# The output bias of three attentions as one more product in the projection's accumulation

## The reference, cut to what matters

```python
def _L2_xattn_ref(query, key, value, Wq, bq, Wk, bk, Wv, bv, Wo, bo):
    q, k, v = query @ Wq + bq, key @ Wk + bk, value @ Wv + bv     # split into 16 heads
    scores = jnp.einsum('bhqd,bhkd->bhqk', q, k) / jnp.sqrt(HEAD_DIM)
    attn = jax.nn.softmax(scores, axis=-1)
    out = jnp.einsum('bhqk,bhkd->bhqd', attn, v)                  # heads joined again
    return out @ Wo + bo

x = x + jnp.tanh(g_xattn[2]) * _L2_xattn_ref(_layernorm(x), ctx_1024, ctx_1024, ...)
```

## Time and profile before

| | us |
|---|---|
| three runs | 1636.18, 1635.72, 1634.01 |
| median | 1635.72 |
| profiled execution: time | 1638.06 |
| profiled execution: span of the trace | 1636.3 |
| PE busy in the span | 1386.8 (85%) |
| DVE busy | 1240.5 (76%) |
| ACT busy | 772.5 (47%) |
| POOL busy | 337.0 (21%) |

### The profile page before, as it was taken

How to read it: one execution, slowest core, us unless ns; L and a number is a source line. 1 busy time by engine, 2 the same in 40 slices (tenths; PEclk the granted TensorE clock), 3 DMA queues, 4 the chain that set the end, 5 groups by cost and what they waited for, 6 DMA issues and landing times.

```text
span 1636.3 us, 25886 instructions
## 1 busy us (share of the span) xinstructions
PE 1386.8 (85%) x9890; PEld 1266.5 (77%) x9890; DVE 1240.5 (76%) x2386; ACT 772.5 (47%) x1318; POOL 337.0 (21%) x278
## 2 busy tenths in 40 slices
PE   4897997798995599999399459968998999999995
PEld 4786895586883599999379358966886888999995
DVE  5696778777896589997379779976886857888773
ACT  4445442113455266666355442325445225676673
POOL 2241001000000157764100000000000013454342
PEclk9898998799998599998699879988998999999997
DMA  4232100000002478886300000000002016777784
GB/s 139 91 104 89 45 1 1 1 0 10 1 1 110 150 211 233 244 224 174 124 1 1 7 0 1 1 10 1 1 1 104 1 65 233 233 214 220 219 241 116
DMA packets 44926, 148.23 MB, mean 91 GB/s; under 512 B 11651, under 2 KB 22582, under 8 KB 35062
## 3 DMA queue, kind: packets, MB, share of 16 engines
q1 hardware_dynamic: 28886, 122.04, 21.9%
q0 software_dynamic: 15936, 24.78, 7.8%
HBM read 126.03 MB, written 22.87 MB: 91 GB/s over the span
## 4 chain that ended last, share of the span: by engine, by line
PE 56%; DVE 26%; ACT 8%; issue 5%; DMA 2%; POOLq 1%; SPq 1%; POOL 0%; ACTq 0%; DVEq 0%
PE PS L307 37%; PE PS L1005 6%; PE PS L966 3%; PE PS L989 3%; DVE RA L1624 2%; PE PS L1240 1%; DVE RA L1693 1%; ACT Y L225 1%; ACT RA L1617 1%; DVE FA L1661 1%; PE PS L998 1%; DVE RA L297 1%; PE PS L982 1%; DVE RA L1673 1%; POOLq L2764 1%
## 5 line engine op out<-in xcount | busy, mean ns | idle before, releaser
L307 PE MATMUL PS<-RA 128*128 128x256 f32 (+3 forms) x6204 | 942.7, 311 | 74.9 <-DVE RA L397 16.2
L307 PEld LDWEIGHTS PS<-RA 128*128 128x128 f32 x6204 | 859.5, 197 | 130.3 <-issue 34.5
L1551 POOL DMA_INDIRECT sum_rows<-Y,KT x78 | 158.6, 2033 | 193.1 <-ACT Y L1592 162.2
L271 POOL TENSOR_TENSOR rstd<-vareps,neghalf 128x4 f32<-128x4 f32 x36 | 36.8, 1023 | 707.2 <-DVE vareps L208 330.0
L1005 PE MATMUL PS<-VBF,FA 128*128 128x136 f32 x1024 | 136.1, 287 | 4.4 <-ACT FA L771 4.2
L1540 POOL DMA_INDIRECT Y<-normed_rows,KT x78 | 89.8, 1151 | 219.7 <-DVE KT L1333 158.5
L1005 PEld LDWEIGHTS PS<-VBF,FA 128*128 128x128 f32 x1024 | 124.8, 192 | 10.3 <-ACT FA L771 6.8
L771 ACT ACTIVATE FA<-PS 128x1024 f32<-128x1024 f32 x64 | 65.7, 1027 | 103.9 <-PE PS L966 103.9
L1570 ACT ACTIVATE FA<-PS,unit_bias 128x256 f32<-128x256 f32 (+1 forms) x184 | 71.7, 445 | 78.2 <-PE PS L307 65.4
L1624 DVE TENSOR_TENSOR RA<-FA,RA 128x2048 fp32r<-128x2048 f32 x46 | 105.2, 2288 | 4.4 <-ACT RA L1584 3.7
L1693 DVE TENSOR_TENSOR RA<-FA,RA 128x1024 fp32r<-128x1024 f32 (+1 forms) x46 | 80.9, 1759 | 24.8 <-ACT RA L1617 24.8
(11 more groups left out here) (295 smaller groups left out, 1874.9 us busy)
## 6 DMA issues: line engine op xcount, KB each, us to landing
FA<-in_eup SPq DMA_DIRECT2D x46, 1024.0 KB, 7.0
FA<-in_edown SPq DMA_DIRECT2D x23, 1024.0 KB, 6.3
FA<-in_edown SPq DMA_DIRECT2D x23, 512.0 KB, 4.1
FA<-in_fside SPq DMA_DIRECT2D x16, 512.0 KB, 3.6
sum_rows<-X SPq DMA_DIRECT2D x2, 2048.0 KB, 7.4
normed_rows<-Y SPq DMA_DIRECT2D x2, 2048.0 KB, 10.2
fp_rows<-FA POOLq DMA_DIRECT2D x6, 352.0 KB, 6.8
FA<-fp_rows SPq DMA_DIRECT2D x1, 2112.0 KB, 11.9
```

The lines of the kernel that those rows point to most:

```text
L307: ins = pe.matmul(dst, stat(a, k), mov(b, k), start=(first and n == 0), stop=(last and n == len(todo) - 1))
L1551: pool.indirect_dma_start(out=sum_rows, in_=rows_out[p][:, t, :], in_offset=None, compute_op=ALU.add, out_offset=bass.IndirectOffsetOnAxis ...
```

## The change

In layers 1 to 3 the bias row is also split in a high and a low part, in partitions 0 and 32 of one tile, and a second tile `sel_r` holds ones in these two partitions and zeros in the others up to 32. One product over partitions 0 to 32 (33 rows, 256 columns) then writes the bias for all 128 tokens into the projection's accumulation, ahead of its six matmuls, and VectorE multiplies PSUM by the gate directly.

```diff
+            sel_raw = fview(8960, P)
+            LOW_ROW = 32
+            bo_r = rview(8192, D)
+            sel_r = rview(8192 + D, P)
...
             def gpsimd(pool):
...
+                else:
+                    pool.memset(sel_raw[0:2 * LOW_ROW], 0.0).then_inc(sel_made, 1)
+                    pool.wait_ge(sel_made, 3 * l - 2)
+                    pool.memset(sel_raw[0:1], 1.0).then_inc(sel_made, 1)
+                    pool.wait_ge(sel_made, 3 * l - 1)
+                    pool.memset(sel_raw[LOW_ROW:LOW_ROW + 1], 1.0).then_inc(sel_made, 1)
+                    pool.wait_ge(sel_made, 3 * l)
...
                 def output_weights_hi():
                     act.wait_ge(wo_in, 16 * (l + 1))
                     act.activation(wo[:, 0], raw_wo, ACT.Copy).then_inc(wo_hi, 1)
+                    if not first:
+                        act.wait_ge(sel_made, 3 * l)
+                        act.activation(sel_r[0:2 * LOW_ROW], sel_raw[0:2 * LOW_ROW], ACT.Copy)
+                        act.wait_ge(bo_in, 16 * l)
+                        act.activation(bo_r[0:2 * LOW_ROW], bo_row[0:2 * LOW_ROW], ACT.Copy).then_inc(bo_hi, 1)
...
                 def output_weights_lo():
...
+                    if not first:
+                        low = slice(LOW_ROW, 2 * LOW_ROW)
+                        dve.wait_ge(bo_hi, l)
+                        dve.tensor_tensor(bo_r[low], bo_row[low], bo_r[low].bitcast(F32), ALU.subtract).then_inc(bo_ready, 1)
...
-                    dve.wait_ge(bo_in, 16 * l)
...
-                            steps(dve.tensor_tensor(tmp, y, bo_row, ALU.add))
                             x = X[:, bass.ds(t, 1), :]
-                            dve.scalar_tensor_tensor(x, tmp.unsqueeze(1), gates[:, l:l + 1], x, ALU.mult, ALU.add).then_inc(fin_done, 1)
+                            dve.scalar_tensor_tensor(x, y.unsqueeze(1), gates[:, l:l + 1], x, ALU.mult, ALU.add).then_inc(fin_done, 1)
...
                         slot.wait(pe, ot_split, -1, 1)
                         if slot.first + slot.p == 1:
                             pe.wait_ge(wo_ready, l + 1)
+                            if not first:
+                                pe.wait_ge(bo_ready, l)
+                        if not first:
+                            pe.matmul(PS[:, 7, D:2 * D], sel_r[0:LOW_ROW + 1], bo_r[0:LOW_ROW + 1], start=True, stop=False)
                         split_matmuls(pe, PS[:, 7, D:2 * D], range(KC), lambda a, k: ot[:, a, k, :],
-                                      lambda m, k: wo[:, m, k, :]).then_inc(y_ready, 1)
+                                      lambda m, k: wo[:, m, k, :], first=first).then_inc(y_ready, 1)
```

More of the change, by code:

```diff
@@ L602, in attention @@
             bo_row = fview(8704, D)
-            tmp = fview(8960, D)
+            sel_raw = fview(8960, P)
+            LOW_ROW = 32
+            bo_r = rview(8192, D)
+            sel_r = rview(8192 + D, P)
             mx = [small[:, p * H:(p + 1) * H] for p in range(2)]
@@ L613, in attention @@
             wo_hi, wo_ready, bq_ready = shared(n_ + "wo_hi"), shared(n_ + "wo"), shared(n_ + "bq")
+            bo_hi, bo_ready, sel_made = (None,) * 3 if first else (shared(n_ + "bohi"), shared(n_ + "bo"), shared(n_ + "sel"))
             neg_ready = shared(n_ + "neg")
```

## The result

The changed kernel took 1665.92 us (median of four, 1664.43 to 1666.69), beside 1635.18 for the kernel before: ratio 1.0182 (95% interval 1.0166 to 1.0198). The forecast was 1657.1, its range ended at 1662. The change made the kernel slower, as forecast, but by 9 us more than the sum. The profiled execution took 1666.69, 28.6 more than the one of before.

A forecast was written before the change was run, and what follows sets the result against it. PE was taken to bound the loops, 4.83 us a slot in layer 1. Ordinary slots 18.0, long 1.6, ends -0.3, beginnings 2.1 sum to 21.4: 1659.5 profiled, median 1657.1 us; range 1646 to 1662.

The forecast's parts named there:

- The product, 0.50: Attention loops of layers 1 to 3: each 33-row product costs PE 0.50 us; 18.0 over 36 ordinary slots.
- The two other prices: Rival prices per product in the loops: 0.12 without array size change (chance 0.09), about 0.30 with part hidden (0.05).
- a hidden way back (0.30): Rival in the loops: return to 128 rows overlaps the wait for L911, price about 0.30, total 1648; chance 0.05.
- Long slots, 0.27: Six slots of layers 1 and 2 with moments: from 5.05 to 5.32, losing 0.27 each, 1.6 in all.
- VectorE's relief: Removed bias addition saves VectorE 0.46 us a tile, limiting the long slots' loss; without effect there, they lose 3.0.
- The ends, -0.3: Last slots of the three loops: added product against VectorE's removed 0.46, together -0.3 us.
- The beginnings, +2.1: Starts of layers 1 to 3: ScalarE's two casts and VectorE's low part delay PE, 2.1 us in all.
- That the rest of the program only shifts: Unstated step: stages outside the attention loops, their beginnings and ends keep their times; layer 1's feed-forward forecast at 0.

The follow-up runs named there:

- e1: Changed kernel with the bias product, its fills and casts over all 128 partitions instead of 33 rows; 1641.45 us, ratio 1.0024.
- e7: Changed kernel with VectorE's bias addition kept, so the bias is added twice; 1666.10 us in a single execution.
- e5: Changed kernel, nothing altered, measured a second time; 1659.13 us, ratio 1.0139.
- e9: Changed kernel, nothing altered, measured a third time; 1664.45 us, ratio 1.0160.
- e4: Changed kernel plus one 256-element and one 64-element addition on VectorE at the end of layer 1's attention; 1664.76 us, ratio 1.0165.
- e10: Changed kernel plus three 256-element additions on VectorE at the end of layer 1's attention; 1664.04 us, ratio 1.0167.
- e3: Kernel before plus six additions on VectorE at the end of layer 1's attention; 1640.13 us, ratio 1.0022.
- e8: Kernel before, but GpSimd adds bias times gate to X's sixteen tiles ahead; no VectorE addition, no product; 1635.92 us, ratio 0.9999.

## Why the prediction was wrong

By its steps:

- **The product, 0.50.** Right: 5.33 - 4.82 = 0.51 and 6.15 - 5.66 = 0.49. The 27-row L2424 was the proper stand-in for 33 rows. The two other prices fall: 0.12 is that of 128 rows (e1), and a hidden way back (0.30) doesn't occur. By the closing table of "TensorE: Matmul & The Clock Gate" in the Trainium skill, where a single product of 32 rows takes the time of one of 128, 33 rows would have cost what e1's 128 do; the trace disagrees by 0.39 a product. "TensorEngine Tiling (Array Packing)" of the Trainium skill says under Key Properties that a change of tiling mode drains TensorE. The trace fits that: both ways together cost 0.39, and neither weight load starts ahead of its product. How much of it is the drain and how much the uncovered load is not shown.
- **Long slots, 0.27.** Right: all 5.33. The reason given, VectorE's relief, was not needed: they are 5.33 with the addition kept (e7). A slot that VectorE had set at 5.05 has cover in one of 5.33 anyway.
- **The ends, -0.3.** Right where it can be read: layer 2's end takes 23.7 us in the profiles of after, e5 and e9, 23.8 in before, for -0.1 forecast. In layer 1 (-0.3 and -0.4 at 508.9) and layer 3 the clock changes in the same microseconds.
- **The beginnings, +2.1.** Right in sum: +0.2 to +0.4 in layer 1 (forecast 0.58), +0.7 in layer 2 (0.77) and +0.8 to +0.9 in layer 3 (0.73), by the starts of PE in after, e5 and e9. The lines of ScalarE, layers 2 and 3, answer to the earlier trace rows:

```profile
816.31 0.63 ACT L717 ACTIVATE RA<-FA 128x512 fp32r<-128x512 f32 x1 [8.48 <-DMA FA<-in_Wo]
816.84 0.29 ACT L720 ACTIVATE RA<-FA 64x128 fp32r<-64x128 f32 x1
817.57 0.42 ACT L722 ACTIVATE RA<-FA 64x256 fp32r<-64x256 f32 x1 [0.43 <-DMA FA<-in_bo]
817.89 1.57 ACT L225 ACTIVATE Y<-X,minus_mean,rstd 128x256 f32<-128x256 f32 x3
...
1124.60 0.63 ACT L717 ACTIVATE RA<-FA 128x512 fp32r<-128x512 f32 x1 [11.23 <-DMA FA<-in_Wo]
1125.14 0.29 ACT L720 ACTIVATE RA<-FA 64x128 fp32r<-64x128 f32 x1
1125.34 0.40 ACT L722 ACTIVATE RA<-FA 64x256 fp32r<-64x256 f32 x1
1125.64 1.04 ACT L764 ACTIVATE RA<-mask 128x1024 fp32r<-128x1024 uint8 x1
```

In layer 3 the mask's cast starts 1.04 behind the weights', 0.51 more than before (0.54 forecast); in layer 2 L225 is 1.58 behind, 1.04 more (0.77 forecast), since the bias row landed 0.43 after ScalarE was ready for it, though PE's start there moved by only 0.7. What was missing is the clock in the slots 0: 0.68 in place of 1.00 in layer 1, +1.3, and 0.68 in place of 0.55 in layer 2, -1.1, for the same work. That some microseconds of a first slot could go at 1.2 GHz was nowhere in the sum.

- **That the rest of the program only shifts.** This is the step that failed, one the sum made without saying so: I multiplied instructions by durations and took TensorE's clock outside the loops as it stood in before. The earlier trace rows showed the clock only inside the loops, where it is full, and I asked for no stretch of the feed-forwards, where the page's PEclk line had slices of 5 to 8 tenths. There the stage's time depends on how the granted clock falls on it: 0.77, 0.80, 0.83 or 0.87 for the same work. In the first measurement that cost 5.6 us; in e5 0.3. The forecast for the profiled execution was 1659.5; e5's was 1657.95, e9's 1660.28, the first 1666.69. So the forecast is a good one of the lower group and has no room for the upper, whose 1664 to 1667 lie above my 1662. That the lower group meets it is in part luck: in e5 the clock gave back 3.4 us behind layer 3's slots and cost 1.7 ahead of layer 3's attention, and neither was in the sum.

A sum of effects that are in every profile of the changed kernel (19.7 in the slots, 1.8 to 2.1 at the beginnings, 1.3 in layer 1's slot 0, less 0.3 at the ends) is 22 to 23; what a measurement has above or below it comes from the clock in work that the change does not touch. Median by median the change cost 30.7, 23.6 and 27.2 us.

**What stays open.** Why the clock of a given stage falls as it does. By their shift at the last 63 us of layer 1's feed-forward, against the point 392, the profiles stand in this order: e9 +9.1 and e5 +9.2 with 0.87, after and e4 +9.4 with 0.77, e10 +9.4 and e7 +9.6 with 0.80. That fits an edge within 0.2 us as well as chance, and no run moved the stage on purpose in this range. e3, which was to bring this about on purpose in the kernel before, did not. Also open is why the casts, which end 20 us ahead of slot 0, leave its clock at 0.68. Not tried was a place for the product beside the scores, whose products have 64 rows anyway; L1016 then writes to the same bank between it and the projection, and whether the product would be cheaper there is not shown.

## What to carry to other kernels

A product of fewer rows among products of 128 costs the change of size both ways (0.39 us here) on top of its own 0.12, and it is paid in every pass of a loop that TensorE bounds: pad it to full height (e1: 0.12), or group the small ones (e2: the second cost 0.12 to 0.14). Work may be moved off VectorE onto TensorE only where TensorE has time; here it bought nothing in the slots. And when a forecast is made from one profile, give each stage at a lowered clock its own range: the same program differed by up to 9.7 us from one execution to another, while its slots repeated to 0.02.

## What the runs showed of the hardware that was not expected

- One 33-row product of 256 columns among 128-row ones: 0.51 us; a second behind it: 0.10 to the next product's start, 0.12 to 0.14 in the slot; one of 128 rows: 0.12.
- The same stage, with the same instructions, spent 16, 21, 25 or 29 us of its last 63 at 1.2 GHz, and thirteen executions of one kernel fell into two groups 4 to 10 us apart.
- A loop's first slot, the same instructions each time, took 4.05 us at a clock of 1.00, 5.3 to 5.4 at 0.68 and 6.43 at 0.55. Layer 1's took 5.4 in all nine profiles with the casts ahead of it and 4.05 in the three without.
- Taking 0.46 us off VectorE in each of 48 tiles (e8) shortened only the slots in which VectorE was last, and was not to be seen in the median (ratio 0.9999).
